# Two PSUM rings of four and three banks in place of three rings, with a new table of places, in a two-layer attention kernel

## The reference

```python
x = x + attn0(layernorm(x))   # 16 heads of 8, biases, softmax(q k^T / sqrt(8)) v, wo, bo
x = x + ffn0(layernorm(x))    # down(silu(gate(x)) * up(x)), hidden 384, int weights / 127
x = x + attn1(layernorm(x))   # fused qkv, q and k RMS-normed per head, softmax, projection
x = x + ffn1(layernorm(x))    # base + router softmax over 8 experts x rank-8 lora
```

## Time and profile before

| | |
|---|---|
| median of 3 runs | 1819.86 us (1817.99 to 1825.17) |
| the profiled execution's own time | 1823.71 us |
| its span, first to last instruction | 1822.0 us |
| PE busy (modelled ends) | 1692.5 us, 93% |
| DVE busy | 1526.1 us, 84% |
| ACT busy | 1410.4 us, 77% |
| POOL busy | 586.3 us, 32% |
| mean granted TensorE clock | 0.986 |

### The profile page before, as it was taken

The page is one execution under the profiler, slowest core; times in us unless marked ns, Lnnn a source line. Parts: engine busy times, 40 slices in busy tenths (PEclk is TensorE's granted clock), DMA queues, the critical chain, the costliest instruction groups (busy, mean ns, idle before and its releaser), DMA issues.

```text
span 1822.0 us, 32452 instructions
## 1 busy us (share of the span) xinstructions
PE 1692.5 (93%) x10962; PEld 648.2 (36%) x10962; DVE 1526.1 (84%) x3347; ACT 1410.4 (77%) x2922; POOL 586.3 (32%) x840
## 2 busy tenths in 40 slices
PE   5999999999999999999999999999999999999994
PEld 2233333434333343333334333343433334334233
DVE  4978889898898989898898888989889897887981
ACT  2778788787878878787787878878787887777872
POOL 4224133151333425124242423315133332423311
PEclk9999999999999999999999999999999999999997
DMA  5222324232142321414133141423214232122310
GB/s 119 66 83 61 112 49 127 52 86 82 43 135 49 118 61 63 104 38 141 49 107 72 49 119 37 128 51 89 82 40 135 49 118 54 43 61 77 89 32 24
DMA packets 164025, 140.97 MB, mean 77 GB/s; under 512 B 40779, under 2 KB 145429, under 8 KB 163861
## 3 DMA queue, kind: packets, MB, share of 16 engines
q1 hardware_dynamic: 162084, 137.92, 28.2%
q10 hardware_dynamic: 1776, 0.98, 0.2%
HBM read 76.99 MB, written 55.57 MB: 73 GB/s over the span
## 4 chain that ended last, share of the span: by engine, by line
PE 67%; ACT 15%; DVE 8%; issue 5%; DMA 2%; POOL 2%; SPq 1%; ACTq 0%; DVEq 0%; POOLq 0%
PE ps L1251 21%; PE ps L1236 16%; ACT probs L741 9%; PE ps L1272 7%; PE ps L1226 7%; PE ps L1183 4%; DVE neg_max L972 4%; ACT xn L747 4%; PE ps L1277 4%; PE ps L1265 3%; PE ps L1316 3%; DVE bn L948 2%; PE ps L1322 2%; DMA rden_all<-rden_rows 1%; DVE x L1009 1%
## 5 line engine op out<-in xcount | busy, mean ns | idle before, releaser
L972 DVE TENSOR_REDUCE neg_max<-ps 128x1 f32<-128x512 f32 x2048 | 1303.4, 680 | 169.5 <-PE ps L1226 164.4
L741 ACT ACTIVATE probs<-ps 128x512 f32<-128x512 f32 x2048 | 1097.9, 595 | 281.2 <-PE ps L1236 279.4
L1226 PE MATMUL ps<-k_stack,q_stack 48*128 48x512 bf16 x2048 | 690.2, 390 | 30.3 <-DVE neg_max L972 26.8
L1236 PE MATMUL ps<-q_stack,k_stack 50*128 50x512 bf16 x2048 | 662.0, 386 | 44.7 <-ACT probs L741 23.1
L1251 PE MATMUL ps<-probs,v_aug 128*32 128x512 f32 x4096 | 549.7, 609 | 2.2
L1236 PEld LDWEIGHTS ps<-q_stack,k_stack 50*128 50x128 bf16 x2048 | 152.7, 94 | 607.7 <-ACT probs L741 369.7
L1226 PEld LDWEIGHTS ps<-k_stack,q_stack 48*128 48x128 bf16 x2048 | 156.9, 93 | 142.9 <-DVE neg_max L972 115.3
L594 POOL TENSOR_TENSOR rstd<-vpe,half_neg 128x4 f32<-128x4 f32 x64 | 64.6, 1009 | 260.1 <-DVE vpe L963 260.0
L615 POOL TENSOR_TENSOR o_raw<-o_raw,rden_all 128x512 f32<-128x512 f32 x64 | 81.5, 1273 | 180.1 <-DMA rden_all<-rden_rows 180.1
L1251 PEld LDWEIGHTS ps<-probs,v_aug 128*32 128x32 f32 x4096 | 80.6, 108 | 140.9 <-issue 85.6
L653 POOL TENSOR_TENSOR coef<-gating,rm 128x64 f32<-128x64 bf16 x64 | 16.7, 293 | 278.6 <-DVE gating L1072 278.6
(11 more groups left out here) (117 smaller groups left out, 1533.3 us busy)
## 6 DMA issues: line engine op xcount, KB each, us to landing
...
```

Source lines behind the costliest of these rows:

```text
L741: act.activation(probs[:, g % RING, :], home("score", (l, b, u)), ACT.Exp).then_inc(exps, 1)
L972: dve.tensor_reduce(neg_max[l][:, pair // 2, col:col + 1], home("max", (l, b, n)), AX.X, ALU.max, negate=True).then_inc(max_taken, 1)
L1226: pe.matmul(home("max", (l, b, m)), q_stack[l][row:row + KROWS, pair, tok:tok + 128], k_stack[l][row:row + KROWS, pair, :], start=True, st ...
L1236: pe.matmul(home("score", (l, b, u)), k_stack[l][row:row + AROWS, pair, tok:tok + 128], q_stack[l][row:row + AROWS, pair, :], start=True, ...
```

## The change

Four things change; the work itself (the instructions, their shapes, the bytes) stays.

- The piece bank is dissolved. Ring A has four banks (0, 1, 2, 7) and holds the scores and 24 kinds of piece; ring V keeps three (3, 4, 5) and holds the maximum tiles, `v1`, `xt3`, `rt` and `kt`. `v0` and `pr0` go from V to A.
- Bank 7 serves the first values, so its first user in the loop waits for these to be read, through `held_before`.
- The numbers in the five tables change, by one to several units.
- Nothing is changed in `GROUPS`; with the new numbers some steps change places on their engines, those of SP and POOL too.

```diff
 PE_AT
-"A": {"m0": -7, "m1": 8, "m2": 25, "m3": 41},
-"P0": {"xt0": -3, "q0": 6, "q0+": 6, "k0": 17, "k0+": 17},
-"P0_fast": {"xt0": 2, "q0": 4, "q0+": 4, "k0": 7, "k0+": 7},
+"A": {"m0": -8, "m1": 8, "m2": 26, "m3": 41},
+"P0": {"xt0": -3, "q0": 9, "q0+": 9, "k0": 15, "k0+": 15},
+"P0_fast": {"xt0": 2, "q0": 6, "q0+": 6, "k0": 12, "k0+": 12},
...
-                "g1+": 33, "u1": 36, "u1+": 36, "g2": 36, "g2+": 36, "u2": 39, "u2+": 39, "dn": 45, "dn+": 46,
-                "xt2": 53, "qka": 55, "qka+": 55, "qkb": 55, "qkb+": 55},
-         "M2": {"qt": 15, "kt": 17, "v1": 19, "v1+": 19},
+                "g1+": 33, "u1": 35, "u1+": 35, "g2": 37, "g2+": 37, "u2": 39, "u2+": 39, "dn": 46, "dn+": 46,
+                "xt2": 54, "qka": 56, "qka+": 56, "qkb": 59, "qkb+": 59},
+         "M2": {"qt": 15, "kt": 15, "v1": 19, "v1+": 19},
...
 ACT_AT
-          "M1": {"tqa": 55, "tqb": 55, "xn1": 25, "xn2": 50, "sq0": 55, "sq1": 56},
+          "M1": {"tqa": 56, "tqb": 59, "xn1": 24, "xn2": 51, "sq0": 57, "sq1": 59},
...
 DVE_AT
-          "S0": {"st0a": 26, "st0b": 29, "mo0": 30, "fa0": 35},
+          "S0": {"st0a": 22, "st0b": 27, "mo0": 30, "fa0": 34},
...
-          "M1": {"add0": 19, "st1": 19, "mo1": 20, "gm0": 31, "gm1": 34, "gm2": 37, "down": 46, "st2": 46,
+          "M1": {"add0": 19, "st1": 20, "mo1": 20, "gm0": 31, "gm1": 33, "gm2": 37, "down": 46, "st2": 46,
...
-                "ga0": 52, "ga1": 58, "ga2": 61, "fin": 69}}
+                "ga0": 54, "ga1": 56, "ga2": 59, "fin": 69}}
 POOL_AT
-POOL_AT = {"A": {"no0": 58, "no1": 76},
+POOL_AT = {"A": {"no0": 64, "no1": 78},
...
-           "P0": {"r1_q0": 26, "r1_k0": 30, "r2_q0": 43, "r2_k0": 38},
+           "P0": {"r1_q0": 32, "r1_k0": 40, "r2_q0": 46, "r2_k0": 43},
...
-           "M1": {"nr0": 64, "nr1": 64, "nr2": 65, "nf1": 25, "um0": 29, "um1": 33, "um2": 44, "nf2": 51},
+           "M1": {"nr0": 66, "nr1": 66, "nr2": 66, "nf1": 22, "um0": 29, "um1": 33, "um2": 40, "nf2": 54},
...
-           "E": {"nf3": 31, "mix": 51}}
+           "E": {"nf3": 26, "mix": 52}}
 SP_AT
-SP_AT = {"A": {"rows0": -5, "rows1": 9, "rows2": 27, "rows3": 42, "den0": 41, "rden0": 59, "den1": 70,
+SP_AT = {"A": {"rows0": -5, "rows1": 9, "rows2": 32, "rows3": 42, "den0": 41, "rden0": 57, "den1": 72,
-         "P0": {"out_p0": 51, "half0_p0": 68, "half1_p0": 97},
+         "P0": {"out_p0": 59, "half0_p0": 62, "half1_p0": 92},
...
-         "M1": {"lr0": 57},
+         "M1": {"lr0": 72},
...
-         "H1": {"cpx2": -14, "half0_p1": 34, "half1_p1": 38},
-         "H1_tail": {"cpx2": 33, "half0_p1": 29, "half1_p1": 61},
+         "H1": {"cpx2": -19, "half0_p1": 39, "half1_p1": 39},
+         "H1_tail": {"cpx2": 43, "half0_p1": 34, "half1_p1": 62},
...
-A_PIECES = ('u0', 'u1', 'u2', 'qt', 'kt', 'xt3', 'qka', 'qkb', 'v1')
-V_PIECES = ('v0', 'pr0')
-A_RING, V_RING, PIECE_RING = (0, 1, 2), (3, 4, 5), (7,)
+A_PIECES = ('u0', 'u1', 'u2', 'qt', 'm0', 'm1', 'm2', 'm3', 'xt0', 'k0', 'xt1', 'xt2', 'ct', 'g0', 'g1', 'g2', 'pr1', 'out', 'dn', 'v0', 'q0', 'pr0', 'qka', 'qkb')
+V_PIECES = ('v1', 'xt3', 'rt', 'kt')
+A_RING, V_RING = (0, 1, 2, 7), (3, 4, 5)
+FIRST_BANK = 7
 def ring_of(kind):
-    if kind == "score" or kind in A_PIECES:
-        return A_RING
-    return V_RING if kind == "max" or kind in V_PIECES else PIECE_RING
+    return A_RING if kind == "score" or kind in A_PIECES else V_RING
 def ring_entries():
-    entries = {A_RING: [], V_RING: [], PIECE_RING: [("begin", 0)]}
+    entries = {A_RING: [], V_RING: []}
 def bank_of(kind, a):
-    return ring[PLACE[kind, a] % len(ring)] if (kind, a) in PLACE else PIECE_RING[0]
+    return ring[PLACE[kind, a] % len(ring)] if (kind, a) in PLACE else FIRST_BANK
 def held_before(kind, a):
-    return ENTRIES[ring][n] if n >= 0 else (None, None)
+    if n >= 0:
+        return ENTRIES[ring][n]
+    return ("begin", 0) if bank_of(kind, a) == FIRST_BANK else (None, None)
```

More of the change, by code:

```diff
@@ L45 @@
             "g0": 2, "u0": 2, "g1": 2, "u1": 2, "g2": 2, "u2": 2}
-PE_AT = {"A": {"m0": -7, "m1": 8, "m2": 25, "m3": 41},
-         "P0": {"xt0": -3, "q0": 6, "q0+": 6, "k0": 17, "k0+": 17},
-         "P0_fast": {"xt0": 2, "q0": 4, "q0+": 4, "k0": 7, "k0+": 7},
+PE_AT = {"A": {"m0": -8, "m1": 8, "m2": 26, "m3": 41},
+         "P0": {"xt0": -3, "q0": 9, "q0+": 9, "k0": 15, "k0+": 15},
+         "P0_fast": {"xt0": 2, "q0": 6, "q0+": 6, "k0": 12, "k0+": 12},
          "V0": {"v0": 15, "v0+": 15},
@@ L50 @@
          "M1": {"pr0": 19, "pr0+": 19, "xt1": 27, "g0": 30, "g0+": 30, "u0": 33, "u0+": 33, "g1": 33,
-                "g1+": 33, "u1": 36, "u1+": 36, "g2": 36, "g2+": 36, "u2": 39, "u2+": 39, "dn": 45, "dn+": 46,
-                "xt2": 53, "qka": 55, "qka+": 55, "qkb": 55, "qkb+": 55},
-         "M2": {"qt": 15, "kt": 17, "v1": 19, "v1+": 19},
-         "E": {"pr1": 22, "pr1+": 22, "xt3": 40, "rt": 45, "rt+": 45, "ct": 65, "out": 69, "out+": 69}}
+                "g1+": 33, "u1": 35, "u1+": 35, "g2": 37, "g2+": 37, "u2": 39, "u2+": 39, "dn": 46, "dn+": 46,
@@ L55 @@
+                "xt2": 54, "qka": 56, "qka+": 56, "qkb": 59, "qkb+": 59},
+         "M2": {"qt": 15, "kt": 15, "v1": 19, "v1+": 19},
+         "E": {"pr1": 22, "pr1+": 22, "xt3": 41, "rt": 45, "rt+": 45, "ct": 65, "out": 69, "out+": 69}}
 ACT_AT = {"A": {"save0": 36, "save1": 67},
-          "P0": {"part0_q0": 7, "part0_k0": 24},
-          "P0_fast": {"part0_q0": 4, "part0_k0": 8},
-          "S0": {"xn0a": 43, "xn0b": 53},
-          "M1": {"tqa": 55, "tqb": 55, "xn1": 25, "xn2": 50, "sq0": 55, "sq1": 56},
@@ L60 @@
-          "M2": {"tv1a": 19, "tv1b": 19, "part0_q1": 17, "part0_k1": 19},
-          "E": {"xn3a": 32, "xn3b": 37, "gexp": 50}}
-DVE_AT = {"A": {"inv0": 43, "inv1": 73},
[1 row of a table removed]
+          "P0": {"part0_q0": 11, "part0_k0": 26},
+          "P0_fast": {"part0_q0": 8, "part0_k0": 15},
+          "S0": {"xn0a": 44, "xn0b": 49},
+          "M1": {"tqa": 56, "tqb": 59, "xn1": 24, "xn2": 51, "sq0": 57, "sq1": 59},
+          "M2": {"tv1a": 19, "tv1b": 19, "part0_q1": 15, "part0_k1": 19},
+          "E": {"xn3a": 31, "xn3b": 38, "gexp": 55}}
@@ L64 @@
+DVE_AT = {"A": {"inv0": 45, "inv1": 73},
[1 row of a table added]
           "V0": {"tv0a": 15, "tv0b": 15},
[2 rows of a table removed]
[2 rows of a table added]
           "E": {"add1": 23, "st3a": 24, "st3b": 26, "mo3": 27, "fa3": 28, "ro0": 45, "ro1": 47, "ro2": 48,
[1 row of a table removed]
-POOL_AT = {"A": {"no0": 58, "no1": 76},
[6 rows of a table removed]
-SP_AT = {"A": {"rows0": -5, "rows1": 9, "rows2": 27, "rows3": 42, "den0": 41, "rden0": 59, "den1": 70,
-                "rden1": 73},
-         "P0": {"out_p0": 51, "half0_p0": 68, "half1_p0": 97},
-         "P0_fast": {"out_p0": 23, "half0_p0": 31, "half1_p0": 63},
-         "S0": {"lx": 7},
-         "M1": {"lr0": 57},
-         "M2": {"out_p1": 16},
-         "H1": {"cpx2": -14, "half0_p1": 34, "half1_p1": 38},
-         "H1_tail": {"cpx2": 33, "half0_p1": 29, "half1_p1": 61},
-         "E": {"store": 76}}
[1 row of a table added]
@@ new lines @@
+POOL_AT = {"A": {"no0": 64, "no1": 78},
[6 rows of a table added]
+SP_AT = {"A": {"rows0": -5, "rows1": 9, "rows2": 32, "rows3": 42, "den0": 41, "rden0": 57, "den1": 72,
+                "rden1": 73},
+         "P0": {"out_p0": 59, "half0_p0": 62, "half1_p0": 92},
+         "P0_fast": {"out_p0": 18, "half0_p0": 37, "half1_p0": 66},
+         "S0": {"lx": 9},
+         "M1": {"lr0": 72},
+         "M2": {"out_p1": 21},
+         "H1": {"cpx2": -19, "half0_p1": 39, "half1_p1": 39},
+         "H1_tail": {"cpx2": 43, "half0_p1": 34, "half1_p1": 62},
+         "E": {"store": 79}}
```

## The result

| | time, us (median, runs) | profiled execution: span, clock | even, odd slot |
|---|---|---|---|
| before | 1819.35 (1812.24 to 1825.17, 20) | 1822.0, 0.986 | 48.0, 59.5 |
| changed | 1822.71 (1816.26 to 1831.13, 20) | 1820.9, 0.977 | 48.9, 59.0 |

The ratio is 1.0023, 95% interval 1.0013 to 1.0033: the changed kernel is 3.4 us slower by the medians, a fifth of a per cent, and the interval leaves out 1. The forecast was a gain, to 1797, with a range of 1760 to 1834. The ratios leave out one execution of the kernel before, of 1909.09 us, and one of e4, of 7834.03, both apart from all others. All lines of the changed kernel are one higher than before.

A forecast was written before the change was run, and what follows sets the result against it. The prediction took DVE as most loaded, idle 12.7 of 107.5 us per batch, with the bound varying by place. Terms summed to −1.7 us per batch, −24 over fourteen, giving 1797 us, with a range of 1760 to 1834.

The forecast's parts named there:

- Queues: Order on SP and POOL: transfers and nf3 ahead of layer 0's four residuals, gating earlier; priced at 0.
- E: Layer 0's next queries and keys, layer 1's keys: qt and kt together, k0 earlier, q0 later; −0.4 us per batch.
- A: Dense stretch: second normalisation (xn1) one unit earlier on ACT shortens DVE's 0.64 us hole; −0.5 us per batch.
- C: gm1 and u1 earlier, g2 later, um0 ahead of no1: second gate product waits less for POOL; −0.4 us per batch.
- D: Query and key projection halves qka and qkb set apart, shrinking DVE's 2.17 us idle time; −0.7 us per batch.
- rival 2: Nothing comes of it: each us saved in one place is waited for in the next; 1820 us, chance 0.20.
- dn: Down projection in one block at step 30, said to be the same PE work; priced at 0, ends ±0.3.
- st0a and st0b earlier: Two steps of statistics moved inside a stretch where DVE has no idle time; priced at 0.
- The rings: Fourth score bank and dissolved piece bank, pieces among scores and maxima; +0.3 us net per batch, ends −5.0 and +2.5.
- Rival 3: Slower: pieces in the maximum ring wait for ACT and idle DVE, 2.5 us per batch; 1838 us, chance 0.14.
- the clean cycle: Stretch of scores, maxima and values alone, about 2.5 us per four units; DVE's work hides the fourth bank, worth nothing.
- rival 4: The clock: new bank order lowers the granted clock in each batch, +1.2 us each; 1814 us, chance 0.06.

The follow-up runs named there:

- e4: Kernel before with only the two new rings, its own places kept; 1832.23 us, ratio 1.0063 to the kernel before.
- e3: Changed kernel with layer 0's first residuals on POOL ahead of nf3 again; 1813.91 us, ratio 0.9964 to the kernel before.
- e9: e3 with layer 0's next queries and keys, layer 1's keys and their ACT readers at old places; 1805.52 us, ratio 0.9922 to the kernel before.
- e11: Changed kernel with POOL's residuals cut from 512 to 16 columns for all batches but the first; 1806.51 us, ratio 0.9930 to the kernel before.
- e7: e3 with the second normalisation and its statistics (xn1, st1) at old places; 1812.06 us, ratio 0.9949 to the kernel before.
- e15: e3 with only the second gate product (gm1) one place later on DVE; 1810.70 us, ratio 0.9940 to the kernel before.
- e8: e3 with gm1, u1, g2 and no1 back at their old places; 1830.68 us, ratio 1.0060 to the kernel before.
- e6: e3 with both halves of the query and key projection in one place again; 1813.20 us, ratio 0.9972 to the kernel before.
- e21: e9 with the down projection alone in two halves again; 1812.33 us, ratio 0.9956 to the kernel before.
- e22: e9 with the next batch's first normalisation at old places on DVE and ACT, nf0 left at 44; 1810.74 us, ratio 0.9941 to the kernel before.
- e5: Changed kernel with the three old rings, new places kept; 1841.68 us, ratio 1.0114 to the kernel before.
- e19: e9 with a layer's last group and attention's own steps, inv0 included, at old places; 1814.84 us, ratio 0.9969 to the kernel before.
- e18: e9 with layer 1's gated-block places outside A, C and D back, dn included; 1815.85 us, ratio 0.9979 to the kernel before.

## Why the prediction was wrong

The sum was −1.7 us per batch, all of it DVE's idle time, with DVE's work unchanged. Measured at full clock: DVE's idle time fell by 1.0 (12.7 to 11.7, even and odd slot together), its work grew by 1.3 (94.8 to 96.1), and the batch by 0.3. Both halves failed.

- **The step that gave the wrong sign** is *Queues*: "nf3 goes ahead of the four residuals of layer 0 … 0". It asked who waits for POOL's results, not who shares a port with POOL. Price: 0.7 us per batch (e3), and up to 0.4 of E's 0.5 by the same mechanism (e9, e11). All collisions: 1.1 per batch (48.9 against 47.8 in e11). Without them the change would still have won 0.7 instead of 1.7.
- **The step that made the gain too large** is the sum of A, C, D and E, −2.0: it took the length of a hole on DVE as the gain of the slot. One by one:
- **A, −0.5: 0.** The hole of 0.64 became two:

```profile
655.01 0.69 DVE L973 TENSOR_REDUCE neg_max<-ps 128x1 f32<-128x512 f32 x1 [0.22 <-PE ps L1227]
```

  the other, 0.42, a few tiles earlier. e7 has the same slots without A. PE is full there, so a gap of DVE that closes opens elsewhere: rival 2's argument.
- **C, −0.4: nothing for the reason given.** The wait of 0.53 grew:

```profile
659.75 0.69 DVE L1022 SCALAR_TENSOR_TENSOR gs<-th,ps 128x512 f32<-128x512 f32 x1 [2.14 <-POOL ht L647]
```

  gm1, a tile earlier, reaches the wait sooner and has no tile ahead of it. That costs nothing either (e15). But C's up and gate projections are what the rings need: 0.8 per batch and the clock (e8). I had "u1 and g2 change places … no work goes", without asking whose reader frees their banks.
- **D, −0.7: the holes as forecast, the gain at most 0.1.** DVE's 2.17 us became 0.84 and 0.66:

```profile
681.31 1.89 DVE L973 TENSOR_REDUCE neg_max<-ps 128x1 f32<-128x512 f32 x3 [0.84 <-PE ps L1227]
...
684.45 1.29 DVE L973 TENSOR_REDUCE neg_max<-ps 128x1 f32<-128x512 f32 x2 [0.66 <-PE ps L1227]
```

  The 1.4 forecast for the sum was 1.5. But two blocks cost PE 1.10 + 1.13 against 1.97, and e6 shows that the slot doesn't follow.
- **E, −0.4: +0.5** (e9). The idle 1.20 us didn't shrink; in the changed kernel 1.32 and 0.34 stand there:

```profile
491.82 1.07 PE L1252 MATMUL ps<-probs,v_aug 128*32 128x512 f32 x8
492.82 1.13 PE L1273 MATMUL ps<-xnt,wk 128*128 128x256 f32 x4
...
494.34 1.29 DVE L973 TENSOR_REDUCE neg_max<-ps 128x1 f32<-128x512 f32 x2 [1.32 <-PE ps L1227]
```
- **dn, 0: −0.3** (e21). "the PE work is the same" was wrong: two blocks took 0.26 more than one.
- **st0a and st0b earlier, 0: −0.3** (e22). DVE has no idle time there, but PE waits there for a bank that DVE frees.
- **The rings, +0.3:** with the old places the odd slot grew by 0.6 (59.5 to 60.1), above the term but within its end; with the new ones the rings are worth −1.4 (e5). A term for the rings apart from the places does not exist. Rival 3's sign is there, an idle time of over 1 us two tiles behind kt (the 1.32 above), but not its cause: PE doesn't wait there, it runs the value products and k0 back to back, and e5, with kt outside the ring of maxima, has 1.57 at the same place. Costing the fourth bank at nothing in the clean cycle was right.
- **Unpriced:** inv0 two places later. The reciprocal's wait for its DMA is 5.6 us before, 2.0 after, and back with the old places (e19); that inv0's place alone does it was not tried.
- **Outcome:** rival 2's number (1820), by a balance of gains and losses rather than by nothing happening; rival 4 in a part, four more odd slots at 0.97. The time lies in the stated range, but the gain that the sum promised did not come: that is luck, for the range was wide enough to hold rivals 2 and 3 as well.

The prices of single steps don't add up to the slots' difference: undone one at a time, dn, the statistics and C cost 1.4 us of an odd slot that is 0.5 shorter in all.

What stays open: what starts the lower clock in one odd slot and not in its equal, the last 0.2 us of e18, and what in e5's even slot makes PE late.
